# 44 pairs of the seventh contraction tile spread over the first four, 34 done in one rounded pass, and the row transposes six banks sooner

## The reference

```
x1[b,s,d] = relu(sum_{h,m} e[b,h,d]  * e[b,m,d] * W1[s,h,m] + b1[s])    s < 128, h, m < 39
x2[b,s,d] = relu(sum_{h,m} x1[b,h,d] * e[b,m,d] * W2[s,h,m] + b2[s])    h < 128, m < 39
z = concat(sum_d x1, sum_d x2);  h = relu(concat(z, dense_ctx) @ W_top1 + b_top1)
h = relu(h @ W_top2 + b_top2);   y = h @ W_top3
```

## Time and profile before

| | |
|---|---|
| median of 3 runs | 1197.61 us (1196.55 to 1199.03) |
| profiled execution | 1195.75 us, its span 1193.7 us, granted clock 0.997 |
| TensorE busy | 1110.4 us (93%), 4507 matmul records |
| VectorE busy | 946.2 us (79%) |
| GpSimd busy | 842.8 us (71%) |
| ScalarE busy | 801.2 us (67%) |
| transfers of SP's queue | 45334 packets, 67.77 MB, 21.4% of the transfer engines' time |

### The profile page before, as it was taken

How to read it: one execution, slowest core, us unless ns; L and a number is a source line. 1 busy time by engine, 2 the same in 40 slices (tenths; PEclk the granted TensorE clock), 3 DMA queues, 4 the chain that set the end, 5 groups by cost and what they waited for, 6 DMA issues and landing times.

```text
span 1193.7 us, 17611 instructions
## 1 busy us (share of the span) xinstructions
PE 1110.4 (93%) x4507; PEld 830.7 (70%) x4507; DVE 946.2 (79%) x2860; ACT 801.2 (67%) x2718; POOL 842.8 (71%) x951
## 2 busy tenths in 40 slices
PE   0059999999999999999999999999999999999998
PEld 0027777777777777777777667777777777777687
DVE  4027888889898989898888668888888888886787
ACT  5016767777777767777777567777677777775674
POOL 6754787788687887788688646887877884453354
PEclk9999999999999999999999999999999999999999
DMA  6256568764876568674876428765676757763342
GB/s 178 37 125 141 110 126 174 153 137 88 178 165 125 117 131 184 135 149 87 183 163 124 98 49 180 164 134 106 130 176 144 147 97 175 168 130 78 66 86 48
DMA packets 73708, 154.70 MB, mean 130 GB/s; under 512 B 14435, under 2 KB 27637, under 8 KB 73606
## 3 DMA queue, kind: packets, MB, share of 16 engines
q0 software_dynamic: 28272, 85.81, 40.6%
q1 hardware_dynamic: 45334, 67.77, 21.4%
HBM read 66.49 MB, written 3.81 MB: 59 GB/s over the span
## 4 chain that ended last, share of the span: by engine, by line
PE 81%; DVE 6%; issue 5%; DMA 2%; ACT 2%; SPq 2%; another core or an unknown queue 1%; DVEq 0%; ACTq 0%
PE bank L682 63%; PE l_acc L666 15%; DVE acc L548 3%; DMA z<-e_rows 2%; ACT prod L421 1%; PE misc L715 1%; PE misc L711 1%; DVE z L508 1%; DVE p2acc L566 0%; DMA e_rows<-e_t 0%; DVE t_sum L556 0%; DVE p L589 0%; DVE t_sum L560 0%; DVE p2l L602 0%
## 5 line engine op out<-in xcount | busy, mean ns | idle before, releaser
L421 ACT ACTIVATE prod<-bank,emb 128x128 f32<-128x128 f32 x2552 | 720.5, 376 | 305.5 <-PE bank L682 272.4
L548 DVE SCALAR_TENSOR_TENSOR acc<-bank,emb,acc 128x128 f32<-128x128 f32 x2184 | 613.3, 340 | 142.7 <-PE bank L682 124.7
L682 PE MATMUL bank<-w2h,x1h 128*128 128x512 f32 (+1 forms) x1280 | 535.4, 418 | 9.4 <-DVE acc L548 6.1
L682 PE MATMUL bank<-w2l,x1h 128*128 128x512 f32 (+1 forms) x1280 | 494.3, 386 | 0.0
L682 PE MATMUL bank<-w2h,x1l 128*128 128x512 f32 (+1 forms) x1280 | 467.0, 427 | 5.5 <-issue 3.8
L310 POOL DMA_INDIRECT emb<-tbl,idx x312 | 310.5, 995 | 82.2 <-issue 76.0
L682 PEld LDWEIGHTS bank<-w2h,x1h 128*128 128x128 f32 x1280 | 240.8, 188 | 107.6 <-issue 56.9
L682 PEld LDWEIGHTS bank<-w2h,x1l 128*128 128x128 f32 x1280 | 240.5, 188 | 89.8 <-issue 35.7
L330 POOL TENSOR_TENSOR tree<-prod 128x640 f32<-128x640 f32 x127 | 240.2, 1892 | 83.2 <-DMA prod<-prod 83.2
L682 PEld LDWEIGHTS bank<-w2l,x1h 128*128 128x128 f32 x1280 | 240.7, 188 | 61.5 <-issue 22.4
L321 POOL DMA_DIRECT2D prod<-prod x127 | 125.1, 985 | 173.7 <-ACT prod L421 171.5
(11 more groups left out here) (96 smaller groups left out, 289.3 us busy)
## 6 DMA issues: line engine op xcount, KB each, us to landing
prod<-prod POOLq DMA_DIRECT2D x127, 640.0 KB
z<-e_rows SPq DMA_DIRECT2D x160, 234.0 KB
z<-e_rows SPq DMA_DIRECT2D x192, 78.0 KB
emb<-tbl,idx POOLq DMA_INDIRECT x312
z<-e_rows SPq DMA_DIRECT2D x32, 156.0 KB
prod<-w_by_h SPq DMA_DIRECT2D x3, 832.0 KB
e_rows<-e_t SPq DMA_DIRECT2D x8, 256.0 KB
wt<-w_top SPq DMA_DIRECT2D x2, 512.0 KB
```

The costliest lines, as they stand in the source:

```text
L421: last = nc.scalar.activation(prod[:, ct % P_RING, i, n * S:(n + 1) * S], bank[:, (ct * NB + k) % RING, n * S:(n + 1) * S], ACT.Copy, scal ...
L548: nc.vector.scalar_tensor_tensor(dst, src, scale, dst if step else b2_row[:, :], ALU.mult, ALU.add).then_inc(v_step, 1)
L682: last = nc.tensor.matmul(out_bank[:, 0:b - a], x, w[:, a:b], start=(n == 0), stop=(n == 2))
```

## The change

The seventh K-tile (`REST = 6`, shifts 18 and 19, 78 pairs) is taken apart. Forty-four of its pairs go as 11 more rows (`EXTRA`) into each of the first four tiles, which then have 128 rows. The other 34 (`REST_RANGES`) are computed in one matmul of 102 rows in the rounded format: each pair has three neighbouring rows, for high by high, high by low and low by high, signed by a constant array `marks`. The weights are prepared once at the start. For each chunk:

- `load_rest_first(f)` loads the first operands, each row three times, to a new buffer `rest` (one for all chunks). It waits until all contractions of chunk f - 1 are done. In SP's order it stands after `load_shifted(f)` and just ahead of `load_shifted(f + 1)`.
- `load_shifted(f)` has 19 transfers: one more for e_rep's rows 117 to 127, one more for each of the first two groups, and four for the second operands.
- In chunks with f % 4 = 0 (`direct`) VectorE multiplies `rest` and z's slot as they stand, both in SBUF. In the others ScalarE first brings `rest` to the PSUM bank e_rep (`copy_first(f + 1)` at g = 26, in place of `copy_rep`), VectorE multiplies at g = 1, and ScalarE then brings the usual rows to e_rep at g = 4 (`SWAP_AT`).
- `round_rest` (ScalarE) writes the rounded product to `rest`, `mix_rest` (VectorE) makes the three kinds of rows of it, with both tensor operands in SBUF.
- The products stand at other units, and the contractions too: for most chunks at 11, 14, 17, 18 (the rounded one), 20, 22 and 25.
- `LIFT_AT` goes from (10, 15) to (4, 9), `LIFT_COPY_AT` from (12, 17) to (6, 11), and the gathers are issued up to two column steps sooner.
- `y` shares memory with `h2`.

```diff
-Z_GROUPS = (range(0, 1), range(1, 4), range(4, 7))
 NF = 7
+REST = NF - 1
+Z_GROUPS = (range(0, 1), range(1, 4), range(4, REST))
...
-MAKE_AT = (1, 4, 7, 10, 13, 16, 19)
-CONTRACT_AT = (7, 10, 13, 16, 19, 22, 25)
+MAKE_AT = (1, 5, 8, 11, 14, 16, 19)
+SWAP_AT = 4
...
-LIFT_AT = (10, 15)
-LIFT_COPY_AT = (12, 17)
+LIFT_AT = (4, 9)
+LIFT_COPY_AT = (6, 11)
 REP_AT = 26
...
+def direct(f):
+
+    return f % CPT == 0
+
+
+def make_order(f):
+    if f == 0:
+        return tuple(range(NF))
+    return (0, 1, REST, 2, 3, 4, 5) if direct(f) else (REST, 0, 1, 2, 3, 4, 5)
...
+def contractions(f):
+
+    if f == 0:
+        return dict(zip((7, 10, 13, 16, 19, 22, 25), range(NF)))
+    if direct(f):
+        return {9: 0, 12: 1, 17: 2, 20: 3, 21: REST, 22: 4, 25: 5}
+    return {11: 0, 14: 1, 17: 2, 18: REST, 20: 3, 22: 4, 25: 5}
+
+
+def round_at(f):
+    return 20 if f == 0 else 11 if direct(f) else 6
+
+
+def mix_at(f):
+    return 21 if f == 0 else 15 if direct(f) else 12
...
-            return min((TILES - 1) * M, -(-M * (ct + 9) // 16))
+            return min((TILES - 1) * M, -(-M * (ct + 9 + min(2, ct // 4)) // 16))
...
+            def load_rest_first(f):
+                sp.wait_ge(et_stored[f // CPT % 2], 64 * (f // CPT // 2 + 1))
+                wait(sp, f_used, NF * f)
+                at = 0
+                for _, a, b in REST_RANGES:
+                    sp.dma_start(rest[3 * at:3 * (at + b - a), :].bitcast(F32), rest_rows(f, a, b - a)
+                                 ).then_inc(in_first, 16)
+                    at += b - a
...
             for f in range(CHUNKS):
+                if f > 1:
+                    load_rest_first(f - 1)
                 if f % CPT == 0:
                     store_rows(f // CPT)
                 load_shifted(f)
+                if f == 0:
+                    load_rest_first(0)
...
+            def copy_first(f):
+                act.wait_ge(in_first, 64 * (f + 1))
+                act.wait_ge(f_made, NF * f)
+                nc.scalar.copy(e_rep[0:3 * N_REST, :], rest[0:3 * N_REST, :].bitcast(F32)).then_inc(first_ready, 1)
+
+            def round_rest(f):
+                act.wait_ge(f_made, NF * f + made_before(f, REST) + 1)
+                nc.scalar.copy(rest[0:3 * N_REST, :], z[0:3 * N_REST, f % 2, REST, :]).then_inc(rest_high, 1)
...
+                    if f < CHUNKS and g == SWAP_AT and not direct(f):
+                        copy_rep(f)
                     if f + 1 < CHUNKS and g == REP_AT:
-                        copy_rep(f + 1)
+                        if direct(f + 1):
+                            copy_rep(f + 1)
+                        else:
+                            copy_first(f + 1)
...
+            def mix_rest(f):
+                rows = F_ROWS[REST]
+                dve.wait_ge(rest_high, f + 1)
+                nc.vector.scalar_tensor_tensor(rest[0:rows, :], z[0:rows, f % 2, REST, :], marks[0:rows, 0:1],
+                                               rest[0:rows, :].bitcast(F32), ALU.mult, ALU.subtract
+                                               ).then_inc(rest_mixed, 1)
...
+                if t == REST:
+                    pe.wait_ge(w_rest_mixed, 1)
+                    pe.wait_ge(rest_mixed, f + 1)
+                    w, x = w_rest[0:rows, :], rest[0:rows, :]
```

More of the change, by code:

```diff
@@ L26 @@
 ROW = D * P
-Z_GROUPS = (range(0, 1), range(1, 4), range(4, 7))
 NF = 7
+REST = NF - 1
+Z_GROUPS = (range(0, 1), range(1, 4), range(4, REST))
 NK = M // 2 + 1
-F_ROWS = [M * min(KP, NK - KP * t) for t in range(NF)]
+EXTRA = P - KP * M
+EXTRA_TILES = 4
+REST_RANGES = ((18, 11, 21), (18, 32, 39), (19, 11, 20), (19, 31, 39))
+N_REST = sum(b - a for _, a, b in REST_RANGES)
+F_ROWS = [P] * EXTRA_TILES + [KP * M] * (REST - EXTRA_TILES) + [3 * N_REST]
 MB = 4
@@ L77, with made_before, pairs @@
 E_SLOTS = 3
+def direct(f):
[4 more added lines that the diff above has]
+    return (0, 1, REST, 2, 3, 4, 5) if direct(f) else (REST, 0, 1, 2, 3, 4, 5)
+def made_before(f, t):
+    return make_order(f).index(t)
+def contractions(f):
[8 more added lines that the diff above has]
+    return 21 if f == 0 else 15 if direct(f) else 12
+def pairs(t):
+    if t == REST:
+        rest = [(h, (h + k) % M) for k, a, b in REST_RANGES for h in range(a, b)]
+        return [(3 * i + c, h, m) for c in range(3) for i, (h, m) in enumerate(rest)]
+    rows = [(k * M + h, h, (h + KP * t + k) % M) for k in range(KP) for h in range(M)]
+    if t < EXTRA_TILES:
+        rows += [(KP * M + h, h, (h + KP * REST + t) % M) for h in range(EXTRA)]
+    return rows
 def pair_weights(w1):
@@ L84, in pair_weights, with rest_marks @@
     for t in range(NF):
[L85 to L90, removed]
-    return ahead, back
+        for p, h, m in pairs(t):
+            ahead[p, t] = w1[:, h, m]
+            if m != h:
+                back[p, t] = w1[:, m, h]
+    return ahead, back
+def rest_marks():
+    marks = np.zeros((P, 3), np.float32)
+    for c, values in enumerate(((0, 1, 0), (1, -1, 0), (0, -1, -1))):
+        marks[c:3 * N_REST:3] = values
+    return marks
 def build(nc, dram, tables, out):
@@ L123, in build @@
         z = sb("z", [P, 2, NF + 1, CH])
+        rest = sb("rest", [P, CH], F32R)
+        w_rest = sb("w_rest", [P, S], F32R)
         x1h = sb("x1h", [P, 2, CH], F32R)
@@ L472, in _ @@
                 for g in range(GB):
+                    if f < CHUNKS and g == round_at(f):
+                        round_rest(f)
                     if f < CHUNKS and g == X1_AT:
@@ L503, in make_f @@
                 rows = F_ROWS[t]
+                part = z[0:rows, f % 2, t, :]
+                if t == REST:
+                    dve.wait_ge(in_second[f % 2], 64 * (f // 2 + 1))
+                    if direct(f):
+                        dve.wait_ge(in_first, 64 * (f + 1))
+                        first = rest[0:rows, :].bitcast(F32)
+                    else:
+                        dve.wait_ge(first_ready, f - f // CPT)
+                        first = e_rep[0:rows, :]
+                    nc.vector.tensor_tensor(part, first, part, ALU.mult).then_inc(f_made, 1)
+                    return
                 dve.wait_ge(rep_ready, f + 1)
```

84 lines of the change are left out of this document (57 added, 27 removed).

## The result

The changed kernel takes 1304.57 us (median of 4 runs, 1298.6 to 1308.44) against 1197.08 us for the kernel before on the same chip: the ratio is 1.0895, 95% interval 1.0859 to 1.0932. The forecast was 1250 us with a range of 1216 to 1290. Slower was right; the size was half of what came.

What follows compares the result with a forecast made beforehand. TensorE, busy 93% of 1193.7 us, was taken as the bound. Pass -21.4, wait +67, start +13, lift -4, VectorE -2 sum to +52.6 us: 1250 us against the median, range 1216 to 1290.

Steps and rivals of the forecast that it cites:

- Step 1, the pass: TensorE's rounded matmul replaces a layer-1 contraction, 0.22 us for 0.91: -0.69 us in each of 31 chunks, -21.4 us.
- Step 2, the new wait: ScalarE's copy at unit 26 waits for loads, TensorE at units 31 and 33: 3.2 us in 21 chunks, +67 us.
- T: Time from first issue to the fourth transfer's landing, taken as 4.2 us (3.2 to 6.2); TensorE waits T - 1.0 us.
- step 5: More work on ScalarE and VectorE fits; slow mixes 0 to +2, taken 0; VectorE's small losses partly go: -2 us.
- the rival given 0.05: TensorE's clock falls to half behind each of 21 waits, 2.5 us lost each: +52, 1302 us; chance 0.05.
- the rival with T at the upper row: T is 6.2 us, so each wait costs 5.2 us, with a start of +20: 1300 us; chance 0.10.
- The MLP chunks, said to hide the wait: In chunks 17 and 29 the MLP's matmuls stretch the same units by over 3 us, so the wait costs nothing.
- Step 3, the start: Before layer 2, chunk 1's copy needs 46 transfers in order instead of 24: +13 us, bounds +7 and +34.
- Step 4, the lift: Lifting six banks sooner removes ScalarE's waits for the loads behind it, of which TensorE had lost part: -4 us.
- The 2 us of relief for VectorE: VectorE's own small losses, for which TensorE's weight loads waited 10.9 us, partly go: -2 us.

Runs made afterwards that it cites:

- fill12: The changed kernel with 12 matmuls into a spare bank ahead of unit 31 in the chunks with the wait: 1289.12 us, ratio 1.0755.
- plain_rows: The changed kernel with the first operands loaded as successive rows instead of each row three times, same bytes, other values: 1261.63 us, ratio 1.0536.
- copy36: The changed kernel with the copy of the first operands at unit 36 of ScalarE's list instead of 26: 1195.22 us, ratio 0.9977.
- hold_gathers: The changed kernel, copy at unit 36, chunk 1 handled as chunk 0, second tile's gathers held until chunk 1's z rows land: 1192.92 us.
- lift_only: The kernel before with the lift six banks sooner and the gathers up to two column steps sooner: 1195.74 us, ratio 0.9988.
- paced: The changed kernel, copy at unit 36, chunk 1 handled as chunk 0, second tile's gathers spread (11 first, then four a step): 1186.57 us.
- paced_even: The changed kernel, copy at unit 36, chunk 1 handled as chunk 0, gathers spread as 16 first, then 3.25 a step: 1187.6 us.

## Why the prediction was wrong

**Step 1, the pass: right.** Chunk 30, which has no wait in either kernel, goes from 32.88 to 32.23 us: -0.65 for the -0.69 forecast.

**Step 2, the new wait: right in place and mechanism, T too small, and one term left out.** The formula held: TensorE waits T - 1.0 us. In chunks 19 and 27, whose clock stays at 1.00, T (first issue to copy) is 4.68 and 4.77 us, and they last 3.66 and 3.70 us more than chunk 30. In fill12 and plain_rows 32 of these chunks have a clock of 1.00; in 27 the excess is T - 1.0 within 0.1 us, in five 0.3 to 0.5 us more. But T was put at 4.2 us, and is 4.79 in the median of the 24 (4.65 to 6.88) and 5.10 in the mean of the 20 chunks. At least 3.05 us of it is issue: transfers that repeat their rows leave SyncE's queue 0.80 us apart, where the e_rep loads of the earlier trace rows suggested 0.4 to 0.5. That is 0.9 us a chunk, 18 us in all.

What failed beside it is that TensorE loses only this. The 20 chunks lose 5.2 us each against the 32.23 us of chunk 30, and T - 1.0 is 4.1 of them. The other 1.1 us, 22 us in all, stands in the 18 chunks that have a stretch at the 1.2 GHz level. Fill12 gets 15.5 us back although its waits are no shorter, so at least that much is the clock; VectorE's mix, in step 5, holds up to 1.7 us of the rest.

**That was the rival given 0.05, and the forecast put it at nothing.** It was argued away with 30 us of full work ahead of the wait. The trace has 1.00 before and 0.58 behind the wait in chunk 3. The Trainium skill ("TensorE: Matmul & The Clock Gate", HAM oscillation) tells of waits for transfers that bring the array back to the slow rate, and the trace agrees, in 18 of the 20 chunks. The rival's price of 2.5 us a chunk was too high, at most 1.1 came. So its total of 1302 us, and the 1300 of the rival with T at the upper row (5.2 us each), are close to the 1304.57 by luck: neither has the causes in the sizes that were measured.

**The MLP chunks, said to hide the wait, don't.** They are 5.4 us longer together where -1.4 was forecast. The wait stands between units 29 and 30 there: 4.3 and 4.4 us, where copy36 has 1.7 in both. The MLP's matmuls stretch the units before the copy as well, and so the contraction that permits the load comes later with them.

**Step 3, the start: failed, on its basis.** It was counted in bytes (94 us); the count of transfers gave 110 us, kept as the upper bound, and the copy's 102.25 lies midway. Chunk 1 begins 22.8 us late for the 16.2 that steps 2 and 3 together gave. SyncE's queue sent one transfer each 1.4 us from 58 to 86 us, while GpSimd's gathers went out (the last at 78 us) and a little beyond, and mostly one each 0.35 to 0.80 us afterwards. Bytes didn't set the pace: in hold_gathers three transfers of 234 KB go out in 1.20 us (from 59.21), and the four of `rest`, 42 to 60 KB each, in 3.05.

**Step 4, the lift: right in size inside this kernel,** -8.3 us in seven chunks, 4.6 from the pass (0.65 each) and 3.7 left for the lift. In lift_only it could not be seen in the median.

**Step 5: nearly right.** The mix takes 0.74 us at best, 1.422 on average and 3.74 at most, as t_sum did; it holds units 17 and 18 back by 0.2 to 0.7 us in four chunks, 1.7 us together. The 2 us of relief for VectorE can't be seen: TensorE's weight loads waited 13.5 us for it, 10.9 before.

Added up, of the 60 us between 52.6 and 112.7: 38 in the 20 chunks (18 and 22, less some 3 that they lost before), 7 in the two MLP chunks, 7 at the start, 6 at the end (this execution), and the 2 us of relief that step 5 counted on.

**What the change is worth.** With the copy moved and chunk 1 changed it reaches 1186.87 us, faster than both kernels. Spreading out the gathers of the kernel before reaches 1188.82 without any of it; the intervals of the two ratios overlap. The two gains didn't add up here: paced and paced_even stay at 1186.57 and 1187.6 us.

## What to carry to other kernels

When an in-order engine is given an instruction that waits for a load, ask what permits that load's issue; here both hung on the last contraction, one unit earlier, and ten units of distance were worth 109 us. Price such a wait as the idle time plus what TensorE does at half rate behind it, here 4.1 and about 1 us. Before work is put off to make room at the start, look for the engine that has to do it later: in the changed kernels GpSimd's gathers, spread out, came back as a wait two or three chunks further on.

## What the runs showed of the hardware

- Four transfers of SyncE's queue that read each row three times took 3.05 us to issue, at best, each 0.80 us behind the one before; the same bytes from successive rows 1.37 us at best (1.6 in the median).
- At the start SyncE's queue sent one transfer each 1.4 us beside GpSimd's gathers (one each 1.25 us), and mostly one each 0.35 to 0.80 us when these were held back. In chunk 0 of hold_gathers it sent 15 of them 0.57 us apart beside gathers of the same pace.
- The copy behind the four loads began 4.65 to 6.88 us after the first issue (median 4.79), and 2.81 to 5.92 (median 3.79) with the plain rows.
- After a wait of 2.6 us TensorE's granted clock was 0.58 over the next 4 us; with 12 matmuls of 2.90 us put into the wait it was 1.00. Two of 20 chunks with such a wait kept the clock at 1.00, and why these two isn't known.
- In chunk 0, ScalarE, VectorE and TensorE stood idle for up to 14 us at a time while long bursts of gathers were issued. The experiments show that these stretches follow the gathers; what was being waited for the profile doesn't say, and it stays open.
